# Unused identity products on TensorE in three stretches where it has nothing to do

## The reference

```
x = x + tanh(g_xattn[0]) * L0_xattn(layernorm(x), ctx, ctx)   # softmax attention, 16 heads
x = x + tanh(g_ffn[0])   * L0_ffn(layernorm(x))               # two transformer layers, see below
x = x + tanh(g_xattn[1]) * L1_xattn(layernorm(x), ctx, ctx)   # mLSTM: gates, decay matrix, 8 heads
x = x + tanh(g_ffn[1])   * L1_ffn(layernorm(x))               # int8 product
```

```
h = h + attn(ln(h)); n = ln(h)
cw = combine_weights(gate(n))        # layer 0: per token; layer 1: per sequence (mean of n)
h = h + sum_e cw[..., e] * (gelu(n @ w1[e] + b1[e]) @ w2[e] + b2[e])
```

## Time and profile before

| what | value |
| --- | --- |
| median of 3 runs | 1160.83 us (1159.97 to 1163.36) |
| the profiled execution's own time | 1158.52 us |
| its span, first to last instruction | 1156.9 us |
| mean granted TensorE clock over the span | 0.906 |
| busy: PE, PEld, DVE, ACT, POOL | 81%, 62%, 70%, 65%, 51% |
| share of the chain that ended last | PE 49%, ACT 15%, DVE 11% |

### The profile page before, as it was taken

The page is one execution under the profiler, slowest core; times in us unless marked ns, Lnnn a source line. Parts: engine busy times, 40 slices in busy tenths (PEclk is TensorE's granted clock), DMA queues, the critical chain, the costliest instruction groups (busy, mean ns, idle before and its releaser), DMA issues.

```text
span 1156.9 us, 30402 instructions
## 1 busy us (share of the span) xinstructions
PE 939.6 (81%) x9773; PEld 716.7 (62%) x9773; DVE 813.3 (70%) x1970; ACT 748.7 (65%) x1892; POOL 585.5 (51%) x783
## 2 busy tenths in 40 slices
PE   3999989899996179999479899966999987999303
PEld 2677767676765169999346666655777776455201
DVE  4599989799986956666479998676222228799873
ACT  2577777688874547777359889753555545688443
POOL 6355545465563045555489997503334320788333
PEclk9899999899998569999769999976999999899755
DMA  5000041000002012222111012500000000111002
GB/s 133 11 17 14 14 129 29 1 2 0 0 1 67 7 42 64 66 66 64 46 33 29 23 28 74 159 1 1 0 0 0 0 10 1 29 46 44 20 0 73
DMA packets 48753, 38.77 MB, mean 34 GB/s; under 512 B 5976, under 2 KB 41284, under 8 KB 48692
## 3 DMA queue, kind: packets, MB, share of 16 engines
q1 hardware_dynamic: 43788, 28.88, 8.6%
q0 software_dynamic: 4320, 8.86, 3.0%
q10 hardware_dynamic: 584, 0.26, 0.1%
HBM read 29.13 MB, written 8.85 MB: 33 GB/s over the span
## 4 chain that ended last, share of the span: by engine, by line
PE 49%; ACT 15%; DVE 11%; issue 8%; POOLq 7%; POOL 4%; DMA 2%; SPq 2%; DVEq 1%; ACTq 0%
PE ps_s L1121 10%; PE ps_o L1121 9%; PE ps_t L1205 8%; PE ps_t L1121 6%; PE ps_a L1121 5%; POOLq L750 5%; PE ps_v L1121 5%; ACT work L873 3%; POOL work L751 2%; ACT shared L864 2%; ACT xcts L839 2%; ACT probs_t L881 1%; PE ps_v L1225 1%; POOLq L740 1%; DMA out_dram<-work 1%
## 5 line engine op out<-in xcount | busy, mean ns | idle before, releaser
L684 POOL TENSOR_TENSOR shared<-kts,kmask 128x512 f32<-128x512 f32 x192 | 240.4, 1274 | 172.7 <-ACT qts L857 81.5
L881 ACT COPY probs_t<-ps_t 128x1024 f32<-128x1024 f32 x96 | 97.2, 1012 | 66.1 <-PE ps_t L1205 66.1
L712 POOL DMA_INDIRECT xg<-x_rows,row_from x71 | 76.5, 1077 | 115.8 <-DVE row_from L1743 51.4
L1575 DVE TENSOR_REDUCE rowmax<-ps_s 128x16 f32<-128x1024 f32 x96 | 116.8, 1217 | 20.4 <-PE ps_s L1121 19.6
L1121 PE MATMUL ps_s<-shared,qts 64*64 64x512 f32 (+1 forms) x1024 | 124.4, 558 | 0.2 <-issue 0.2
L1578 DVE TENSOR_TENSOR work<-ps_s,rowmax 128x1024 f32<-128x1024 f32 x96 | 117.6, 1225 | 3.3
L1205 PE MATMUL ps_t<-ident,work 128*128 128x128 f32 x768 | 105.5, 282 | 15.0 <-ACT work L873 13.5
L1121 PE MATMUL ps_o<-shared,probs_t 128*64 128x18 f32 x3072 | 107.7, 213 | 7.6 <-ACT probs_t L881 7.6
L1121 PEld LDWEIGHTS ps_o<-shared,probs_t 128*64 128x64 f32 x3072 | 98.1, 138 | 20.2 <-ACT probs_t L881 10.1
L1205 PEld LDWEIGHTS ps_t<-ident,work 128*128 128x128 f32 x768 | 88.0, 144 | 23.3 <-ACT work L873 23.2
L873 ACT ACTIVATE work<-work 128x1024 f32<-128x1024 f32 x96 | 100.9, 1051 | 1.4 <-DVE work L1578 1.2
(11 more groups left out here) (388 smaller groups left out, 2358.0 us busy)
## 6 DMA issues: line engine op xcount, KB each, us to landing
y_rows<-work SPq DMA_DIRECT2D x71, 64.0 KB, 1.6
w<-in_L_ffn_e_w_dram SPq DMA_DIRECT2D x2, 2048.0 KB, 11.2
ctx_dup<-in_ctx_dram SPq DMA_DIRECT2D x64, 64.0 KB, 2.3
x_res<-in_x_dram SPq DMA_DIRECT2D x4, 512.0 KB, 6.6
ctx_in<-in_ctx_dram SPq DMA_DIRECT2D x32, 64.0 KB, 1.8
x_rows<-h_all SPq DMA_DIRECT2D x1, 2048.0 KB, 10.0
out_dram<-work SPq DMA_DIRECT2D x16, 128.0 KB, 1.8
xg<-x_rows,row_from POOLq DMA_INDIRECT x71, 2.6
```

What stands on the lines that cost most here:

```text
L684: i = pool.tensor_tensor(km[:, par, g, :, :], kts[:, par, g:g + 1, :].to_broadcast([P, 8, SEQ]), kmask[:, :, :], ALU.mult)
L712: pool.indirect_dma_start(xg[:, t % XBUFS, :], None, x_d, bass.IndirectOffsetOnAxis(row_from[:, t:t + 1], 0)).then_inc(xg_loaded[t % XBUFS ...
L881: nc.scalar.copy(probs_t[:, par, :], ps_t[:, :]).then_inc(S["pts_ready"], 1)
L1575: V.tensor_reduce(rowmax[:, par, :], s3, AXX, ALU.max).then_inc(S["max_ready"], 1)
```

## The change

TensorE gets a function that multiplies a bfloat16 identity with the causal mask into `ps_s`, n times. Nothing reads the result, and no wait or semaphore is added. It is called at nine points: after pieces 2 to 6 of the inversion with 3 products each and after piece 7 with 14; with 14 after the `at_place` products; with 14 after the last gate product and with 8 after the cumulating product.

```diff
+            def keep_streaming(n):
+
+                for _ in range(n):
+                    mm(ps_s[:, 0:512], identb[:, :], causal[:, :, :].rearrange("p a b -> p (a b)"))
+
...
             for k in range(PIECES):
                 invert(k)
+                if k >= PIECES // 4:
+                    keep_streaming(3 if k < PIECES - 1 else 14)
             pipeline(pe, [(1, turn_transpose, XBUFS), (3, turn_second, XBUFS), (1, turn_hidden)], NTURN)
...
                 i.then_inc(S["quad_out"], 1)
 
+            keep_streaming(14)
             pe.wait_ge(S["tables_ready"], 1)
             pipeline(pe, [(3, quad_second), (1, quad_hidden)], NQUAD, 2)
...
             i.then_inc(S["gates_ps"], 1)
+            keep_streaming(14)
 
             pe.wait_ge(S["gate_link"], 2)
             mm(ps_v[:, 0:NT * MH], block_tri[:, :], lsig[:, :, :].rearrange("p t h -> p (t h)")
                ).then_inc(S["csum_ps"], 1)
 
+            keep_streaming(8)
             pe.wait_ge(S["avec_ready"], 1)
```

## The result

| | us |
|---|---|
| kernel after, median of 20 runs | 1152.19 (1150.65 to 1161.95) |
| kernel before, median of 20 runs beside them | 1159.50 (1155.56 to 1165.88) |
| ratio of the two | 0.9954, 95% interval [0.9935, 0.9973] |
| profiled execution of after | 1161.95 (span 1160.3) |

The change makes the kernel 0.46% faster; 0.5% was forecast. Set against the 1160.83 of the prediction the ratio gives 1155.5 us.

A forecast was written before the change was run, and what follows sets the result against it. TensorE bounds turns and mLSTM, GpSimd the quads; their starts run at the lower clock. Turns 1.9, quads 1.3, gates 1.9 sum to 5.1 us; with 0.4 for late clock changes, 1155.3 us from 1160.83; 8-in-10 range 1152.3 to 1159.7.

The forecast's parts named there:

- Turns: First turns after the inversion: upper clock shortens the chain to the steady turn; 2.8 us in full, 1.9 taken.
- Rival 1: Streams too short: clock falls in the idle rest behind them at two of three places; 1159.4 us, chance 0.20.
- with the clock rising within the first 3 us: Stream behind piece 7: then it ends before 412.8, ahead of the first transpose, at cost 0.
- Quads: Second routing's first quad: hidden step 3.77 to 1.99 us, GpSimd's third quad 1.8 us earlier; 1.3 taken.
- feared rest: Before the first quad: up to 2.5 us idle left behind the stream at the upper clock, which might lose it.
- Gates: mLSTM start: cumulating product saves 0.5 us, first three decay steps 1.4; 1.9 us taken in full.
- 3.9 us: Gates, sign of being right: third decay step's mask about 3.9 us after lsig's wait ends, not 7.3.
- Costs: All streams: hidden in the waits, cost taken as 0; behind piece 7 bounds 0 and 1.1 us.
- Spacing: Within a stream: the next product starts 0.43 us later at the lower clock, 0.21 at the upper.
- Rival 3: Streams: products don't overlap in a row, each costs its own 0.6 us at the lower clock; 1166.6 us, chance 0.05.
- Rival 4: Streams don't raise the clock: minus 1.1 us at the turns, minus 1.0 at the gates; 1162.9 us, chance 0.05.
- Rival 2: Gain swallowed: clock is up but what follows isn't TensorE's; only some 2 us left, 1158.8 us, chance 0.07.

The follow-up runs named there:

- e5: The changed kernel plus the same product in six more waits (12, 60, 3 each, 4 and 11, 9, 8); ratio to the kernel before 0.9975.
- e10: The changed kernel unedited, run again for another profile; ratio to the kernel before 0.9930.
- e9: The changed kernel unedited, run again for another profile; ratio to the kernel before 0.9974.
- e7: The changed kernel without the products between pieces, plus 8 behind the last quad; ratio to the kernel before 0.9938.
- e8: The changed kernel without the products between pieces, nothing else edited; ratio to the kernel before 0.9891 from 2 runs.
- e1: The changed kernel with all 65 added products kept but 4 columns each instead of 512; ratio to the kernel before 0.9984.

## Why the prediction was right

**The sum.** 5.1 us were forecast against the profiled execution; the ratio's 0.46% are 5.3 us. The measured median, 1152.19, lies 0.1 us under the lower end of the range, but the kernel before had moved by 1.3 us as well. The stretches give about the same. Without streams T averages (13.86 + 12.91 + 12.68) / 3 = 13.15, Q 13.28, G (13.80 + 14.98 + 14.50) / 3 = 14.43; the four executions of the changed kernel average 11.81, 11.49 and 12.28. That is 1.3 + 1.8 + 2.15 = 5.3 us, 0.45%, or 4.9 us with e5's T. That the sum comes so near 5.1 is in part luck: the terms are off in both directions and cancel, and the averages of T and G rest on three or four executions that lie up to 1.7 us apart.

- *Turns*, 1.9 taken, full value 2.8. The pair shown has 2.8 to the tenth, by the steps that were named. The average is 1.3 (0.9 with e5), since in three of the five executions with the threes and the 14 the clock falls at the first turn. Rival 1 is true at this one place and in part of the executions. The step that was off is "with the clock rising within the first 3 us": in all five it had risen before, by the threes (in e5 and e10 it had fallen once between them and was up again), and the 2.0 us of rest, which the prediction gave as the upper bound, follow from that.
- *Quads*, 1.3 taken: 1.8 in every execution of the change, the upper bound. The 1.97 us (2.0 said) and that nothing more comes behind it held. The feared rest was there in some executions (2.23 us in e9) and did no harm. (The "up to 2.5 us" doesn't follow from the prediction's own numbers: 14 at the upper clock from 790.0 on end at 792.9, 3.6 us ahead of 796.48; the 2.5 needs part of the stream at the lower clock.) As for why it did no harm, behind it TensorE is busy without a pause, behind the one at the turns it isn't. That this is what decides is argued, not shown.
- *Gates*, 1.9 taken: 1.5 in the pair, 2.15 against the average without streams. In the pair the first decay step starts 0.4 us earlier (0.5 said), and from there to the third it is 1.1 us less (1.4 said). A wait was left out there: the third step doesn't only wait for GpSimd's spread but for VectorE's shift of the first, 0.53 us (the row above). The "3.9 us" in the list of what would show it doesn't fit the prediction's own saving, 7.27 - 1.9 = 5.4; measured, 987.82 to 993.56 is 5.7 us.
- *Costs*, 0 taken: none in after. Where the 14 behind the last piece ran at the lower clock (e7, e8) the first transpose came half a us late, inside the bounds of 0 and 1.1. At double length the cost appears at all three places.
- *Spacing*: 0.43 and 0.21 in the streams too. Rival 3 falls. So does, for this case, what the Trainium skill states in "TensorE: Matmul & The Clock Gate", section "Back-to-back issue gap": at about 131 ns a product the estimate for 14 was 1.8 us; they last 3.18.
- *Rival 4*, no rise of the clock: refuted at each place (e1 against after). *Rival 2*, gain swallowed: refuted, since what follows T, Q and G lasts the same in both kernels (134, 145 and 80 us).

**What stays open.** What decides, at equal instructions and an idle rest of 2.04 to 2.08 us, whether the clock falls at the first turn: no experiment here varies it alone. Whether leaving out the threes gains in the total: T is 0.5 us shorter on average than in the four executions of the changed kernel (0.9 with e5), from four executions each way, and the ratios don't separate it. Why the second self-attention takes 6 to 17 us longer on the other chips.

## What to carry to other kernels

A stream that only holds the clock pays where three things meet: TensorE is, or paces, what comes right behind the wait; the wait ends at data that the stream can't delay; and nothing gives the time back. Size it by the clock that it starts at, so that it ends close before the data and never far behind it, above all where thin work follows: at the turns a rest of up to 0.8 us kept the clock in four of four executions with 14, one of 2.0 to 2.3 us in two of five (and with 28 and no rest it fell at the first output step); ahead of the dense quads up to 2.2 us kept it in eight of eight. A small change of this sort is judged by the time between fixed instructions over several executions; one profile can show a term at its full size or at none.

## What was not expected of the hardware

- Nearly the same idle rest at the turns kept the clock in two executions (2.04 us each) and lost it in three (2.06, 2.08 and 2.30), with the same instructions right around it; ahead of the quads 2.02 and 2.23 us kept it.
- Executions of the kernel before differ by ten us beside after and by up to 16.5 us on another chip (1166.38 to 1182.92), and at least part of it is where the clock falls: 159.60 to 169.80 in after had 9.21 us of TensorE busy and still ran at 0.50.
- The clock also rises later or earlier under equal load: the kernel before needed 13.80 us for G in one execution and 14.98 in another.
- It can also fall between the pieces, with the same instructions as those at which it had risen (e10, 407.19).
